# Rows of softmax scales in a cross-attention kernel: 32x32 transposes on VectorE in place of TensorE transposes and ScalarE copies

## The reference, cut to what matters

```python
kv = jnp.concatenate([xn, ln_lat], axis=1) @ Wkv
k, v = jnp.split(kv, 2, axis=-1)
weight = jnp.einsum('bhld,bhnd->bhln', q * scale, k * scale)
weight = jnp.where(full_mask[:, None, None, :], weight, neg)
weight = jax.nn.softmax(weight.astype(jnp.float32), axis=-1)
out = jnp.einsum('bhln,bhnd->bhld', weight, v)
```

## Time and profile before

| | |
|---|---|
| median of 3 runs | 882.67 us (881.75 to 884.01) |
| profiled execution | 880.55 us |
| its span | 878.8 us |
| TensorE matmul, busy | 844.0 us (96%) |
| TensorE weight load, busy | 785.3 us (89%) |
| VectorE, busy | 575.0 us (65%) |
| ScalarE, busy | 440.7 us (50%) |
| GpSimd, busy | 350.7 us (40%) |
| granted TensorE clock, mean | 0.997 |

### The profile page before, as it was taken

How to read it: one execution, slowest core, us unless ns; L and a number is a source line. 1 busy time by engine, 2 the same in 40 slices (tenths; PEclk the granted TensorE clock), 3 DMA queues, 4 the chain that set the end, 5 groups by cost and what they waited for, 6 DMA issues and landing times.

```text
span 878.8 us, 17399 instructions
## 1 busy us (share of the span) xinstructions
PE 844.0 (96%) x6331; PEld 785.3 (89%) x6331; DVE 575.0 (65%) x1536; ACT 440.7 (50%) x1023; POOL 350.7 (40%) x364
## 2 busy tenths in 40 slices
PE   2999999999999999999999999999999999998997
PEld 2989999999999999999999999999977689987885
DVE  7455656566576878755575665777776656656885
ACT  4565554545556465544545545445525424434552
POOL 5723624645353674646355344314301310003442
PEclk9999999999999999999999999999999999999999
DMA  5456346566566767566665764788577757932220
GB/s 186 164 174 201 112 137 204 180 209 218 201 241 232 265 215 267 221 212 218 229 229 202 235 226 145 275 342 261 175 279 306 307 232 287 351 130 92 101 49 25
DMA packets 71110, 183.04 MB, mean 208 GB/s; under 512 B 6337, under 2 KB 19569, under 8 KB 65009
## 3 DMA queue, kind: packets, MB, share of 16 engines
q1 hardware_dynamic: 70928, 181.90, 58.7%
q10 hardware_dynamic: 96, 0.02, 0.0%
HBM read 130.00 MB, written 50.86 MB: 206 GB/s over the span
## 4 chain that ended last, share of the span: by engine, by line
PE 79%; DVE 8%; DMA 4%; issue 3%; ACT 3%; POOL 1%; SPq 1%; DVEq 0%; ACTq 0%; POOLq 0%
PE pJ L1656 14%; PE pJ L1657 14%; PE pJ L1658 14%; PE pV L1786 7%; PE pS L1764 4%; PE pT L1772 3%; PE pS L1772 3%; PE pT L1764 2%; PE pS L1656 2%; PE pS L1658 2%; PE pS L1657 2%; DMA w_split<-wvst 1%; PE pX L1687 1%; DVE late L1613 1%; PE pV L1656 1%
## 5 line engine op out<-in xcount | busy, mean ns | idle before, releaser
L1656 PE MATMUL pJ<-WV,XT 128*128 128x256 f32 x544 | 158.5, 291 | 0.0
L1657 PE MATMUL pJ<-WV,XT 128*128 128x256 f32 x544 | 153.8, 283 | 0.0
L1658 PE MATMUL pJ<-WV,XT 128*128 128x256 f32 x544 | 153.7, 283 | 0.0
L858 ACT ACTIVATE SP<-SP,xneg 128x768 f32<-128x768 f32 (+1 forms) x96 | 85.8, 896 | 119.6 <-DVE xneg L1235 119.6
L1656 PE MATMUL pJ<-XT,WK 128*128 128x384 f32 (+1 forms) x384 | 127.2, 331 | 2.9 <-DVE VT L1131 2.4
L1657 PE MATMUL pJ<-XT,WK 128*128 128x384 f32 (+1 forms) x384 | 125.4, 326 | 0.0
L1658 PE MATMUL pJ<-XT,WK 128*128 128x384 f32 (+1 forms) x384 | 125.4, 326 | 0.0
L1131 DVE TENSOR_TENSOR KT<-pJ,KT 128x384 fp32r<-128x384 f32 x96 | 51.3, 535 | 90.2 <-ACT KT L835 89.5
L1656 PEld LDWEIGHTS pJ<-WV,XT 128*128 128x128 f32 x544 | 104.1, 191 | 0.5 <-issue 0.2
L1657 PEld LDWEIGHTS pJ<-WV,XT 128*128 128x128 f32 x544 | 104.2, 192 | 0.0
L1658 PEld LDWEIGHTS pJ<-WV,XT 128*128 128x128 f32 x544 | 104.0, 191 | 0.0
(11 more groups left out here) (382 smaller groups left out, 2154.2 us busy)
## 6 DMA issues: line engine op xcount, KB each, us to landing
WS<-w_split SPq DMA_DIRECT2D x14, 2048.0 KB, 8.3
WV<-wv_split SPq DMA_DIRECT2D x20, 1024.0 KB, 7.6
WK<-wk_split SPq DMA_DIRECT2D x40, 512.0 KB, 4.5
w_split<-wkst SPq DMA_DIRECT2D x40, 512.0 KB, 3.2
w_split<-wvst SPq DMA_DIRECT2D x40, 512.0 KB, 3.9
XA<-w_split SPq DMA_DIRECT2D x4, 2048.0 KB, 12.9
xraw<-in_ctx SPq DMA_DIRECT2D x7, 768.0 KB, 6.7
wk_split<-WK SPq DMA_DIRECT2D x8, 512.0 KB, 3.8
```

The costliest lines, as they stand in the source:

```text
L858: ac.activation(SP[:, I % 2, h, 0:w], SP[:, I % 2, h, 0:w], ACT.Exp, bias=xneg[:, I % 2, h:h + 1], scale=XSC, accum_out=total).then_inc(c_ ...
L1656: te.matmul(dst, a(HI), b(HI), start=start, stop=False)
L1657: te.matmul(dst, a(HI), b(LO), start=False, stop=False)
L1658: return te.matmul(dst, a(LO), b(HI), start=False, stop=stop)
```

## The change

VectorE now makes the rows itself, in `turn_scales(I)`, between `stats` and the masked maxima. alpha and linv lie in one tile, scales. For each group of 32 partitions a (four of them) it copies the 2 or 4 columns of scales into a tile of 32 partitions, columns[:, column, a]. Then it transposes 32x32 blocks of which each is one such column read 32 times (stride 0), once to the partitions 0 to 31 of scl and once to 32 to 63, and last copies partitions 0 to 63 of scl to 64 to 127. `link` is a wait of VectorE on its own last instruction. TensorE's transposes, ScalarE's copies, the semaphore c_rb and the waits that guarded pX are gone; ScalarE's `rescale` now waits on c_scl, which VectorE sends.

```diff
-        alpha = sb("alpha", [P, 2, 2])
+        scales = sb("scales", [P, 2, 2, 2])
-        linv = sb("linv", [P, 2, 2])
+        columns = sb("columns", [32, 4, 4])
+        alpha, linv = scales[:, :, 0, :], scales[:, :, 1, :]
...
                 if m >= 2:
                     act.wait_ge(c_lu, m - 1)
-                    act.wait_ge(c_rb, m - 1)
+                    act.wait_ge(c_scl, m - 1)
...
-            def scale_rows(I):
-
-                R = I // PAIRS
-                if R % SPLITS == 0:
-                    return
-                m = I - (R // SPLITS + 1) * PAIRS
-                act.wait_ge(c_rb, m + 1)
-                if m > 0:
-                    act.wait_ge(c_mg, I)
-                if R % SPLITS == SPLITS - 1 and pair_index(I) > 0:
-                    act.wait_ge(c_of, pair_index(I))
-                w = 256 if R % SPLITS == 1 else 512
-                ac.activation(scl[:, :, :, :].rearrange("p s h t -> p (s h t)")[:, 0:w], pX[:, 0:w], ACT.Copy).then_inc(c_scl, 1)
...
+            def turn_scales(I):
+
+                R, par = I // PAIRS, I % 2
+                if R % SPLITS == 0:
+                    return
+                m, n = I - (R // SPLITS + 1) * PAIRS, R % SPLITS
+                if n == 2:
+                    dve.wait_ge(c_rec, pair_index(I) + 1)
+                if m > 0:
+                    dve.wait_ge(c_mg, I)
+                if n == 2 and pair_index(I) > 0:
+                    dve.wait_ge(c_of, pair_index(I))
+                for a in range(4):
+                    last = ve.tensor_copy(columns[:, 0:2 * n, a], scales[32 * a:32 * a + 32, par, 0:n, :].rearrange("p s h -> p (s h)"))
+                link(last)
+                column = columns[:, 0:2 * n, :].rearrange("p c a -> p (c a)").unsqueeze(2).broadcast_to([32, 8 * n, 32])
+                rows = lambda p0, p1: scl[p0:p1, 0:n, :, :].rearrange("p s h t -> p (s h t)")
+                for a in range(2):
+                    last = ve.transpose(rows(32 * a, 32 * a + 32).rearrange("p (c t) -> p c t", t=32), column)
+                link(last)
+                ve.tensor_copy(rows(DH, P), rows(0, DH)).then_inc(c_scl, 1)
...
                 if 3 <= C8 < CHUNKS:
                     stats(C8)
+                turn_scales(I)
...
-                if scaled_before(C, k) > 0:
-                    pe.wait_ge(c_scl, scaled_before(C, k))
...
-            def rows_of_scales(I):
-
-                R, par = I // PAIRS, I % 2
-                if R % SPLITS == 0:
-                    return
-                m = I - (R // SPLITS + 1) * PAIRS
-                pe.wait_ge(c_alpha, m + 1)
-                if R % SPLITS == SPLITS - 1:
-                    pe.wait_ge(c_rec, pair_index(I) + 1)
-                if m > 0:
-                    pe.wait_ge(c_scl, m)
-                pe.wait_ge(c_xh, turned_before(I))
-                for h in range(2):
-                    last = te.transpose(pX[:, L * h:L * h + L], alpha[:, par, h:h + 1].broadcast_to([P, P]), ident[:, :])
-                    if R % SPLITS == SPLITS - 1:
-                        last = te.transpose(pX[:, 256 + L * h:256 + L * h + L], linv[:, par, h:h + 1].broadcast_to([P, P]), ident[:, :])
-                last.then_inc(c_rb, 1)
...
-                rows_of_scales(I)
...
-            pe.wait_ge(c_scl, 4 * PAIRS)
```

More of the change, by code:

```diff
@@ L203, in perceiver_layer @@
         c_s = sem("c_s"); c_ttr = sem("c_ttr"); c_neg = sem("c_neg"); c_exp = sem("c_exp"); c_alpha = sem("c_alpha")
-        c_lu = sem("c_lu"); c_rec = sem("c_rec"); c_rb = sem("c_rb")
+        c_lu = sem("c_lu"); c_rec = sem("c_rec")
         c_t = sem("c_t"); c_th = sem("c_th"); c_tl = sem("c_tl"); c_o = sem("c_o")
@@ L384, in steps_of @@
             return None
[L386 to L394, removed]
         @block.sync
@@ L953, in _ @@
                     value_hi(G, I % 2)
-                scale_rows(I)
                 if I + 3 < PAIRS:
```

## The result

The changed kernel takes 912.81 us (median of 4, 912.05 to 913.94) against 883.34 us for the kernel before (4 runs): a ratio of 1.035, 95% interval 1.033 to 1.037. The prediction was 891.9 us with a range of 881 to 905, slower with a chance of 0.68. The direction came true; the size was about three times what the sum gave, and the time lies above the range. The profiled execution of the change spans 912.1 us, that of before 878.8: 33.3 us to explain, where the sum had 9.2. (The medians differ by 29.5 us: the profiled execution of the change was the slowest of its four, and that of before, at 880.55 us, was under all its others.)

A forecast was written before the change was run, and what follows sets the result against it. TensorE, busy 96% of the span, was taken to bound the kernel. Terms -2.2 + 4.0 + 3.2 + 1.5 + 2.7 = +9.2 us took the profiled 880.55 to 889.8, and the median, 2.1 above, to 891.9 us; range 881 to 905.

The forecast's parts named there:

- the undisturbed block: VectorE's added copies, transposes and links per iteration: 2.0 us in rounds 1 and 4, 2.66 in rounds 2 and 5.
- overlap: Rival: VectorE's copies and transposes overlap, so the block takes 2.2 and 1.5 us; sum +1.9, 884.6 us; chance 0.17.
- a block within the hole: Rival: the new work stays in VectorE's idle time and the kernel is faster, 877.0 us at 1.6 us; chance 0.14.
- half rate: Rival: VectorE's transposes of four-byte elements run at half rate, blocks 3.7 and 2.5 us, 910 us; chance 0.11.
- the hole: VectorE's idle time before the first masked maximum, 2.03 us in iteration 44 and 2.01 in 45, where the work goes.
- the tail: From iteration 47, without scores or hole: TensorE's waits for XA's low half and for weights move by 2.66; +2.7 us.
- the pairs: Even iteration with the next odd one in rounds 2 and 5: each costs 1.05 us, five pairs 5.3.
- Step 1: VectorE's unseen holds: a join's add takes 0.315 us in the middle, 1.341 at worst; kept out of the sum.
- Step 2: Iterations with statistics: 11 and 35 have 1.44 us of cover; 15 loses 1.1, 19 costs +3.2, 23 +1.5.
- Step 3: TensorE's granted clock: the prediction's sum had no term or size for it.
- Step 4: TensorE sheds 96 transposes, 10.4 us on the path, plus a 0.6 us wait in iteration 20; weight load costed at nothing.
- the second rival: The work stays in VectorE's hole and the kernel is faster; break-even near 2.1 us in rounds 2 and 5; chance 0.14.

The follow-up runs named there:

- reduce_copies: Changed kernel with each block's four tiny copies written as a tensor_reduce over an axis of one element, same values: 900.4 us, ratio 1.021 against the kernel before.
- no_rows: Changed kernel without turn_scales, scl set to 1.0 once: 874.7 us, ratio 0.992 against the kernel before.
- filler: reduce_copies plus twelve unread TensorE transposes between second value product and key products of iterations 15 and 19: 899.2 us, ratio 1.020 against the kernel before.
- after_narrow: Changed kernel with GpSimd's later weight splits and context low halves cut to 8 columns (output not the layer's): 892.06 us, ratio 1.011 against the kernel before.

## Why the prediction was wrong, and where it was right

By its own terms, in us, from the lengths of the iterations in the profiled executions; the middle column is the change with its blocks at their plain length.

| term of the sum | predicted | reduce_copies | the change |
|---|---|---|---|
| rounds 1 and 4 but 11, 15, 35 (13 iterations) | -2.9 | -2.85 | +0.73 |
| 11 and 35 | -0.4 | +1.66 | +1.63 |
| 15 | +1.1 | +4.06 | +2.51 |
| rounds 2 and 5 but 19, 23, 47 (13 iterations) | +4.0 | +6.19 | +16.53 |
| 19 | +3.2 | +4.73 | +4.60 |
| 23 | +1.5 | +3.87 | +4.77 |
| from 47 on | +2.7 | +2.42 | +2.00 |
| sum (with rounds 0, 3 and the start) | +9.2 | +20.2 | +33.3 |

**Right:** the price of the undisturbed block (1.90 and 2.57 us; transposes 0.43 and 0.70, last copy 0.29 and 0.42, four copies end to start in 0.68), which sets the rivals of overlap, of a block within the hole and of half rate aside; the gain per iteration, where nothing else waits (no_rows); the kind of wait that takes the place of the hole (VT, 19 times; 3.5 us in 19, where over 4 was said); and nearly the tail (2.0 us for 2.7, though the new wait is for the normalised rows and that for XA fell from 0.86 to 0.50). In reduce_copies the pairs cost on the whole what was said: 40 with 41 +1.05, the forecast's own number, 42 with 43 +1.39, 20 with 21 +1.42, but 16 with 17 only +0.43 and 44 with 45 +2.28. That 40 with 41 agrees to the last digit is in part luck: the even one kept nothing (-0.23 was said) and the odd one cost 1.05 (1.28 was said).

**Step 1 that failed:** "VectorE is sometimes held by something that its own length does not show; that is not in the sum and widens the range upward." It was the largest term. The change and reduce_copies differ by 12.4 us in their medians (13.1 in the profiles), and by nothing but the form of the four copies (an unheld reduce is 0.01 us shorter than an unheld copy). Of the 24.1 us between the sum and the change that is over half; of the other 11.0, 8.9 lie in the five iterations of step 2. The rows for it were there before: the join's 1.341 in the earlier trace rows, and GpSimd's timeline in before, busy from 287.88 to 292.26, through the very hole of iteration 18 that the block was to fill. A range's width was no place for it: it was a price with a cause, and the cause stood in a timeline that wasn't read.

The Trainium skill (SBUF — State Buffer, section "Who interferes with whom") states that VectorE's copies in its two-port modes, and its operations with both inputs in SBUF, contend with GpSimd, and that whoever issues first keeps the pair of ports for the whole instruction. The runs agree: copies, negations (0.17 to 1.16 us) and operations on two SBUF tiles (0.28 to 1.37 in the join) are held, and transposes, reduces, reciprocals and what reads PSUM are not. The prediction cited another page and missed this one.

**Step 2:** "two (11 and 35) have one value tile more ahead of the keys", and with it the other iterations with statistics. The table's predictions for the five make 5.4 us together, and reduce_copies has 14.3. They fail for three reasons. First, a longer chain. In 11 the 1.44 us of cover did hold for the first low half (it ends at 210.92 in the change, and the first key product starts), but the negation is 1.56 us later too, and behind it stand the exponentials, ScalarE's next high half and the next low half:

```profile
212.58 0.58 ACT L833 ACTIVATE VT<-pJ 128x512 fp32r<-128x512 f32 x1
...
213.19 0.69 DVE L1107 TENSOR_TENSOR VT<-pJ,VT 128x512 fp32r<-128x512 f32 x1 [1.04 <-ACT VT L833]
...
213.94 0.44 PE L1655 MATMUL pJ<-XT,WK 128*128 128x384 f32 x1 [0.59 <-DVE VT L1107]
```

(ScalarE, VectorE and TensorE in iteration 11 of the change.) The second key product waits for a chain that the prediction did not follow. Second, in 15 and 19 of reduce_copies the wait brought the lower clock, 1.4 and 1.6 us by filler. Third, GpSimd again: it holds VectorE's negations and merges as well, and these two of iteration 14 of reduce_copies (0.17 and 0.41 us when free, 0.17 and 0.83 in before) help to make VectorE late for 15:

```profile
248.51 0.90 DVE L1211 TENSOR_SCALAR xneg<-mx 128x2 f32<-128x2 f32 x1
...
250.59 1.51 DVE L1264 TENSOR_TENSOR Oacc<-Oacc,scl 128x256 f32<-128x256 f32 x1
```

The statistics of 15 end 5.92 us into the iteration (4.84 in before), and those of 23 at 7.73 (5.69). In after_narrow they end at 4.84 and 5.76, and there 15 costs 1.60 and 23 1.93 us, near the 1.1 and 1.5 of the prediction; 11 with 35 cost 1.64 there too. From iteration 8 on all instructions of VectorE together lie some 8 us over their plain lengths in before, some 17 in reduce_copies and some 31 in the change: beside the held copies, VectorE's old instructions also met GpSimd's work more often once the block stood among them.

**Step 3:** TensorE's clock was no term at all. Summed over iterations 8 to 45, length times what the granted clock lacks is 8.5 us in the change (19, 21, 23 and 43 stand at 0.90, 0.82, 0.91 and 0.89), 3.4 in reduce_copies and nothing in before. That is an upper bound of what it cost, and it lies within the iterations of the other two steps, not beside them. The earlier trace rows gave no warning: a wait of 0.88 us left the clock at 1.00.

**Step 4:** the 10.4 and 0.6 us gained. Measured alone they are 7.1. The rest was lost where TensorE then waits for something else: the key weights in 42 and 44, VectorE in 15, 19, 20 and 42. That the weights' load was costed at nothing failed here, and with no block to make OF late: in no_rows TensorE reaches iteration 42 4.95 us sooner than in before (583.94 for 588.89), and the load is issued only 2.58 us sooner (589.08 for 591.66).

Together the runs make a curve. A part for VectorE of 0, of 0.88 and 1.42 (ScalarE does the rest), of 1.90 and 2.57 us, and the last with the copies held, gives 874.7, 879.7, 900.4 and 912.8 us: the first 1.4 us cost 5, the next 1.2 cost 21. The break-even of the second rival, near 2.1 us, was put too high: an estimate on a straight line between the second and the third point has it near 1.5.

Open: why some waits bring the lower clock and others of the same length do not; how much of the excess in 44 and 45 belongs to the join, which GpSimd still holds in reduce_copies; and what 19 would cost at the full clock (4.42 us in after_narrow, at 0.81). None was tried apart.

## What to carry to other kernels

Before an instruction goes into an engine's idle time, lay the other engines' timelines over the same stretch: an idle VectorE beside a busy GpSimd takes a transpose or a reduce, but not a copy, a negation or an operation on two SBUF tiles at its plain length. A hole is worth its length once, and what is beyond it comes back as a wait, and at times as that wait's clock; so give the hole only what needs the engine (here the transposes) and put the rest on one with slack (ScalarE, 47% busy). And a range's width should hold no term whose cause a row already names.

## What had not been expected of the hardware

- A copy of 32 x 4 fp32 elements, 0.16 us long, took up to 1.27 us beside GpSimd (32 x 2: 1.24); the reduce of the same elements took 0.152 at most, in the same place.
- TensorE did more work in less time: twelve added transposes (1.47 us) ahead of a wait's end shortened two iterations by 1.4 and 1.6 us.
- A wait of 1.73 us (iteration 15 of reduce_copies) brought the lower clock, one of 2.38 us (its 23) did not.
- ScalarE's copies between groups of partitions take 0.20 us for 32 x 2 or 32 x 4 elements, 0.42 for 64 x 256 and 0.63 for 64 x 512, longer than VectorE's 0.29 and 0.42 for the last two, and cost less where they stand (879.7 against 900.4 us).
